# Seven value products from the third group on, and a late slot for three of four dense weight sums

## The chip, the cores and the metric

The kernel runs on one core of a Trainium2 chip. The metric is device time in microseconds (us) of one execution; three runs of the kernel before gave 767.40, 767.96 and 769.08 us, median 767.96 us.

## The reference

```python
def attention(x):                       # x is (2, 1024, 1024), already layer-normed
    x = conv1d(x, conv_w, width 3, 'SAME') + conv_b        # -> 3 * 256 columns
    q, k, v = split(x, 3); blocks of 128 tokens
    qh, kh, vh = q @ wq + bq, k @ wk + bk, v @ wv + bv      # 16 heads of 64
    p = softmax(causal(qh @ kh.T / 8))                      # within a block
    o = (p @ vh) @ wo + bo
    return o @ proj_w + proj_b
def ffn(x):                             # x is layer-normed again
    y = x @ W_base.T + b_base
    z = x @ A[active]; contribs = z @ B[active] * 2         # 4 active experts of rank 8
    alpha = softmax(log(prior + 1e-12) + x @ router_W.T + router_b)
    return y + sum(contribs * alpha)
x = x + attention(layernorm(x))
x = x + ffn(layernorm(x))
```

Everything is float32. All products are made so: an operand is split into a high part (`..._hi`, a rounded type that TensorE takes fast) and the rest (`..._lo`), and hi·hi, hi·lo and lo·hi are summed in PSUM.

## The kernel before

Up to about 250 us the convolution runs; from about 560 us on the second layer (the "dense" one) does. The change lies between them, in the attention.

The 2048 tokens are 8 **groups** of 256 tokens (e or g = 0 to 7), and the 16 heads are 8 pairs. A pair of heads in a group is a step jj; two of them are a **double step** D, `attention_pair(D)`, which every engine has as a function of its own. Group g owns the double steps 4g to 4g+3. Here ds 9 means D = 9. In a double step TensorE (PE) does, in this order: scores of two steps, head outputs of two older ones, transposes ("turns") of the probabilities, queries and keys of a new step, a *unit* (k = 0), queries and keys of the other step, a unit (k = 1), and the output sums. PE's matmuls of the scores (L2043) open a double step, so the time from one such start to the next is its length.

A *unit* is a part of the group's big products. In ds 4g+1 and 4g+2 the units are the **values** of group g (vh, a 256x256 by 256x1024 product); in ds 4g+3 and 4g+4 they are the output projection of group g-1, whose first matmul waits for `a_lo` of that group. The values exist in two forms, and the number `SEVEN` says from which group on the second is used:
- four units of two chunks each: 8 hi/lo products of three matmuls with 512 columns, 24 matmuls (`values`, L63 to L65);
- seven products of 2x2 blocks in place of eight, after Winograd's form of Strassen's scheme: 21 matmuls (`seven_values`, L1976 to L1978). Products 1 to 3 stand in ds 4g+1, 4 to 7 in ds 4g+2. VectorE adds them up into `vf` (L1455, L1458), and PE waits for its additions, since the seven share two PSUM banks.

The second form needs sums of blocks. For the values of group e VectorE makes four sums of the tokens' blocks in ds 4e-1 (`value_sums`, L1465 to L1470), ScalarE rounds them (`vs_hi`, L1043) and VectorE makes the rest (`vs_lo`, L1475) at the end of ds 4e. Once in the kernel GpSimd (POOL) makes four sums of the weight's blocks (`wv_again`, L800), ScalarE rounds them (`vt_hi`, L1061), and GpSimd makes the rest (`vt_lo`, L806), which product 3 of the first group of this form waits for (`pool_step` 10).

Beside it VectorE (DVE) prepares the sums of the dense layer's weights, 16 of them (k = 0 to 15): `weight_sum` (L1587) writes `t_raw`, ScalarE rounds it (`t_hi`, L1055), `low_sum` (L1599) makes the rest one sum later, and SyncE stores both to HBM. Sum k is due in double step 8 + 4(k/4) + (0, 0, 1, 2)[k mod 4]. In a double step VectorE has an early slot for it (after `heads_low`, L1430, ahead of the unit's additions) and a late slot (after the reciprocals and the units). Each engine works through its instructions in this written order.

GpSimd's other work here: the probabilities times the reciprocals (L784), the rest `c_lo` of the next group's tokens (L765, last in ds 4g+2 and 4g+3), and the bias sums of the residual (L775, two at the head of ds 4g+3). VectorE in ds 4g+3 first masks the scores of one step (L1418, four instructions), then makes `a_lo` (L1437), for which the projection on PE waits.

Of the kernel before, what the change touches and what calls it, by code (L numbers as in the profile page):

```python
# [19 lines left out]
WC = W // P  # L20
# [67 lines left out]
def network(nc, ident, x, conv_w, conv_b, wq, wk, wv, wo, pw, bq, bk, bv, bo, pb, w_base, b_base, lora_a, lora_b, router_w, router_b,  # L88
# [45 lines left out]
    DG = NP // 2  # L134
# [4 lines left out]
        e, n = ((g - 2, 2), (g, 0), (g, 2), (g - 1, 0))[q]  # L139
        return (q in (1, 2), e, n + k) if 0 <= e < NG else None  # L140

    SEVEN = 3

    def v_before(e):

        return VT * min(e, SEVEN) + 7 * max(0, e - SEVEN)

    def v_left(e, n, k):

        return v_before(e) + ((n + 1) if e < SEVEN else ((3, 2), (7, 6))[n // 2][k])  # L150

    def v_low(e):

        return WC + 5 * (e - SEVEN)

    def pair_of(D):

        return (2 * D, 2 * D + 1) if 0 <= D < ND else ()
# [26 lines left out]
    TFIRST, TSUMS = 8, 16  # L185
# [17 lines left out]
    def sum_at(k):  # L203
        return TFIRST + DG * (k // 4) + (0, 0, 1, 2)[k % 4]

    def sums_in(D, late):
        return [k for k in range(TSUMS) if sum_at(k) == D and (k % 4 == 1) == late]

    W_LAST = TFIRST + DG * (TSUMS // 4) + 1

# [40 lines left out]
    with ExitStack() as ctx:  # L251
# [135 lines left out]
        s = {n: sp.sem(n) for n in names}  # L387
# [55 lines left out]
        def value_raw(i):  # L443
            return value_block(*((0, 0), (0, 1), (1, 1), (1, 0))[i])

        def value_sum(part, i):
            return (vt_hi, vt_lo)[part][:, i] if i < 3 else (wv_hi, wv_lo)[part][:, 0, BANK:2 * BANK]
# [52 lines left out]
        def _(sync):  # L500
# [135 lines left out]
            def attention_step(g, i):  # L636
# [7 lines left out]
                if i == 7 and g + 2 < NG:  # L644
                    if g == 0:
                        sync.wait_ge(s["c_stored"], 16 * (MC + 1))
                    sync.wait_ge(s["c_lo_ready"], 2 * (g + 1))
                    if g + 1 >= SEVEN:
                        sync.wait_ge(s["v_low_step"], v_low(g + 1) + 4)
# [91 lines left out]
        def _(pool):  # L741
# [18 lines left out]
            def c_low(g, h):  # L760
                m = slice(3 * h, 3 * h + 3)
                pool.wait_ge(s["c_hi_ready"], 2 * (g - 1) + h + 1)
                wait(pool, s["qk_done"], NP * (g - 1))
                wait(pool, s["v_done"], v_before(g - 1))
                pool.tensor_tensor(c_lo[:, g % 2, m], c_raw[:, m], c_hi[g % 2][:, m], ALU.subtract).then_inc(s["c_lo_ready"], 1)  # L765

            def tile_power(t):
                pool.wait_ge(s["fvar_ready"], t + 1)
                r = rstd[:, t % 2] if t < BLOCKED else mv[:, t % 2, 1:2]
                pool.tensor_tensor(r, vareps[:, t % 2], mhalf[:], ALU.pow).then_inc(s["frstd_ready"], 1)  # L770

            def bias_sum(e, k):
                if k == 0:
                    pool.wait_ge(s["xr_loaded"], 16 * (e + 2))
                pool.tensor_tensor(xr[:, k], xr[:, k], pb_r[:], ALU.add).then_inc(s["xb_ready"], 1)  # L775

            def attention_pair(D):
                g, q = D // DG, D % DG
                if 0 <= g - 1 < NG - 1 and q == 3:
                    bias_sum(g - 1, 0)  # L780
                    bias_sum(g - 1, 1)
                for jj in pair_of(D - SC):
                    pool.wait_ge(s["rrec_ready"], jj + 1)
                    pool.tensor_tensor(pr[:, jj % 4], pr[:, jj % 4], rrec[:, jj % 4].unsqueeze(2).to_broadcast([P, UN, P]), ALU.mult).then_inc(s["p_ready"], 1)  # L784
                if 0 < g and g + 1 < NG and q in (2, 3):
                    c_low(g + 1, q - 2)
                if D == DG * SEVEN - 4:
                    value_weight_sums()
                if D == DG * SEVEN:
                    low_value_sums()  # L790
                if D in (27, 29):
                    tile_power((D - 27) // 2)

            def value_weight_sums():

                b11, b12, b21, b22 = (value_block(i, j) for i in range(2) for j in range(2))
                pool.wait_ge(s["wv_loaded"], 32)
                for k, (to, left, right) in enumerate(((b11, b12, b11), (b12, b22, b12), (b22, b22, b11), (b21, b21, b22))):
                    pool.wait_ge(s["pool_step"], 2 + k)
                    pool.tensor_tensor(to, left, right, ALU.subtract).then_inc(s["pool_step"], 1)  # L800

            def low_value_sums():

                for i in range(4):
                    pool.wait_ge(s["v_high_ready"], WC + i + 1)
                    pool.tensor_tensor(value_sum(1, i), value_raw(i), value_sum(0, i), ALU.subtract).then_inc(s["pool_step"], 1)  # L806

            pool.memset(mhalf[:], -0.5).then_inc(s["pool_step"], 1)
# [16 lines left out]
            for D in range(ND + 1):  # L825
                attention_pair(D)
# [57 lines left out]
        def _(act):  # L884
# [90 lines left out]
            def queries_keys(J):  # L975
                i = J % NP
                act.wait_ge(s["qk_done"], J + 1)
                wait(act, s["sc_done"], J - 1)
                act.activation(qf[:, J % 2], qk_acc(J)[:, 0], ACT.Identity, bias=bqk_c[:, 0, i:i + 1])
                act.activation(kf[:, J % 2], qk_acc(J)[:, 1], ACT.Identity, bias=bqk_c[:, 1, i:i + 1]).then_inc(s["qk_ready"], 1)  # L980
# [6 lines left out]
            def heads_out(jj):  # L987
                act.wait_ge(s["o_done"], jj // 2 * 2 + 2)
                wait(act, s["a_step"], jj - 1)
                act.activation(oT_hi[:, jj % 2], op[:, jj % 2].rearrange("p b t -> p (b t)"), ACT.Identity,  # L990
                               bias=bv_c[:, jj % NP:jj % NP + 1]).then_inc(s["oT_hi_ready"], 1)
# [11 lines left out]
            def a_high(e):  # L1003
                act.wait_ge(s["a_step"], NP * (e + 1))
                wait(act, s["yy_done"], YT * e)
                for d in range(WC):
                    a = act.activation(by_plane(a_hi[:, d]), planes_of(ap_[:, d]), ACT.Identity, bias=bo_c[:, d:d + 1])
                a.then_inc(s["a_hi_ready"], 1)

            def attention_pair(D):  # L1010
                g, q = D // DG, D % DG
                if q == 3 and 0 <= g - 1 < NG:
                    a_high(g - 1)
                for jj in pair_of(D - PV):
                    heads_out(jj)
                if D == 2:
                    queries_keys(2 * D)
                if D == ND:
                    exponentials(2 * (D - SC))
                for jj in pair_of(D - TR):  # L1020
                    turned_out(jj)
                for h in range(2):
                    if D < ND and D != 2 and h == 0:
                        queries_keys(2 * D)
                    if pair_of(D - SC) and (D, h) != (ND, 0):
                        exponentials(2 * (D - SC) + h)
                    if 0 < g and g + 1 < NG and (q, h) in ((1, 0), (3, 0)):
                        c_high(g + 1, q // 2)
                    if D < ND and D not in (2, 3, 4) and h == 1:
                        queries_keys(2 * D + 1)  # L1030
                if D == 2:
                    c_high(1, 0)
                    c_high(1, 1)
                for k in sums_in(D, False) + sums_in(D, True):
                    high_sum(k)
                if D == DG * SEVEN - 3:
                    high_value_sums(range(2))
                if D == DG * SEVEN - 1:
                    act.wait_ge(s["v_done"], v_before(SEVEN))
                    high_value_sums(range(2, 4))  # L1040
                if q == 3 and SEVEN <= g + 1 < NG:
                    act.wait_ge(s["v_low_step"], v_low(g + 1) + 4)
                    act.activation(vs_hi[:], vs_raw[:], ACT.Copy).then_inc(s["v_high_ready"], 1)  # L1043
                if D in (1, 2):
                    k = D - 1
                    act.wait_ge(s["wo_pw_loaded"], 32)
                    act.activation(wo_hi[:, 4 * k:4 * k + 4], wo_raw[:, 4 * k:4 * k + 4], ACT.Copy).then_inc(s["wo_hi_ready"], 1)
                if D in (4, 5):
                    act.wait_ge(s["wo_pw_loaded"], 32)
                    act.activation(pw_hi[:, D - 4], pw_raw[:, D - 4], ACT.Copy).then_inc(s["pw_hi_ready"], 1)  # L1050
# [6 lines left out]
            def high_value_sums(which):  # L1057

                for i in which:
                    act.wait_ge(s["pool_step"], 3 + i)  # L1060
                    act.activation(value_sum(0, i), value_raw(i), ACT.Copy).then_inc(s["v_high_ready"], 1)  # L1061
# [192 lines left out]
        def _(dve):  # L1254
# [216 lines left out]

            def low_values(e):

                dve.wait_ge(s["v_high_ready"], WC + 4 + e - SEVEN + 1)
                dve.tensor_tensor(vs_lo[:], vs_raw[:], vs_hi[:], ALU.subtract).then_inc(s["v_low_step"], 1)  # L1475

            def unit_out(D, k):
# [895 lines left out]
```

## Time and profile before

| | |
|---|---|
| median of 3 runs | 767.96 us |
| profiled execution | 767.93 us |
| its span | 766.2 us |
| clock granted to TensorE | 0.999 of full speed |
| PE busy | 745.9 us (97%) |
| VectorE busy | 584.6 us (76%) |
| ScalarE busy | 458.7 us (60%) |
| GpSimd busy | 186.1 us (24%) |
| DMA | 124.12 MB, mean 162 GB/s |

The span goes from the first to the last instruction; 1.7 us of the time lie around it. A row of a timeline gives start, duration, engine, line, operation, output and inputs, and in brackets how long the engine sat idle before and who released it. A recorded duration of VectorE includes what it waits inside the instruction.

### The profile page before, as it was taken

The page shows a single profiled execution, that of the slowest core. Times are in us where ns is not written, and L with a number is a line of the kernel's source. Part 1 is how long each engine was busy: PE and PEld are TensorE (multiplying, and loading weights), DVE is VectorE, ACT ScalarE, POOL GpSimd, SP SyncE. Part 2 cuts the span into 40 slices and gives each one's busy share as a digit, 9 for nine tenths or more (in the row PEclk, how much of TensorE's full clock was granted, in tenths as well). Part 3 has the DMA queues.
Part 4 walks back from the last instruction along what each step waited for, and adds up shares of the span by engine and source line. Part 5 has one row for each costly group of instructions (what it writes and reads, how often), then busy time and mean ns, then how long its engine had stood idle before and what let it go on. Part 6 is the DMA issues. An engine that isn't in the chain of part 4 may idle for free.

```text
span 766.2 us, 15175 instructions
## 1 busy us (share of the span) xinstructions
PE 745.9 (97%) x5311; PEld 670.7 (88%) x5311; DVE 584.6 (76%) x1573; ACT 458.7 (60%) x1189; POOL 186.1 (24%) x212
## 2 busy tenths in 40 slices
PE   4999999999999999999899999999999999999997
PEld 3898888888888889999899998999988899999997
DVE  6999996879888885767876776576688567777784
ACT  5963443334433787788677777777794155566530
POOL 2300100000000123645462626253430211222200
PEclk9999999999999999999999999999999999999999
DMA  8836843444445244163536364513357986433402
GB/s 323 300 119 188 259 118 130 173 165 145 165 143 215 111 167 118 56 205 104 177 101 212 89 218 155 188 48 111 114 195 224 353 219 208 134 124 134 159 29 83
DMA packets 64848, 124.12 MB, mean 162 GB/s; under 512 B 11908, under 2 KB 32516, under 8 KB 63365
## 3 DMA queue, kind: packets, MB, share of 16 engines
q1 hardware_dynamic: 62756, 115.81, 45.9%
q0 software_dynamic: 2016, 7.34, 2.4%
q8 instruction: 43, 0.70, 0.4%
q14 instruction: 33, 0.26, 0.1%
HBM read 87.92 MB, written 34.80 MB: 160 GB/s over the span
## 4 chain that ended last, share of the span: by engine, by line
PE 87%; DVE 5%; DMA 3%; ACT 3%; issue 1%; SPq 0%; DVEq 0%; ACTq 0%
PE net_psum L63 13%; PE net_psum L65 13%; PE net_psum L64 13%; PE net_psum L1941 11%; PE net_psum L2224 5%; PE net_psum L2226 5%; PE net_psum L2225 5%; PE net_psum L2043 4%; PE net_psum L2055 4%; PE net_psum L2067 3%; PE net_psum L2097 2%; PE net_psum L2098 2%; PE net_psum L2099 2%; DMA t_scratch<-t_low 1%; PE net_psum L1925 1%
## 5 line engine op out<-in xcount | busy, mean ns | idle before, releaser
L784 POOL TENSOR_TENSOR pr<-pr,rrec 128x512 f32<-128x512 f32 x64 | 66.5, 1042 | 195.3 <-DVE rrec L1426 194.2
L971 ACT ACTIVATE pr<-pr,negmax 128x128 f32<-128x128 f32 x256 | 99.6, 400 | 1.3 <-DVE negmax L1418 1.3
L1941 PE MATMUL net_psum<-ua,wa 128*128 128x256 f32 x384 | 83.8, 379 | 0.6 <-DVE ua L1308 0.6
L1941 PEld LDWEIGHTS net_psum<-ua,wa 128*128 128x128 f32 x384 | 72.6, 190 | 10.4 <-issue 0.8
L928 ACT ACTIVATE w_hi<-raw 128x1024 fp32r<-128x1024 f32 x24 | 25.5, 1063 | 85.4 <-PE net_psum L65 76.7
L63 PE MATMUL net_psum<-x_hi,w_hi 128*128 128x512 f32 x192 | 76.4, 398 | 0.0
L64 PE MATMUL net_psum<-x_lo,w_hi 128*128 128x512 f32 x192 | 76.2, 397 | 0.0
L65 PE MATMUL net_psum<-x_hi,w_lo 128*128 128x512 f32 x192 | 75.6, 394 | 0.0
L63 PE MATMUL net_psum<-c_hi,wqk_hi 128*128 128x256 f32 x256 | 74.1, 289 | 0.0
L64 PE MATMUL net_psum<-c_lo,wqk_hi 128*128 128x256 f32 x256 | 71.6, 280 | 0.0
L65 PE MATMUL net_psum<-c_hi,wqk_lo 128*128 128x256 f32 x256 | 71.5, 279 | 0.0
L1418 DVE CUSTOM_DVE_ANT_0 pr<-net_psum,mask 128x128 f32<-128x128 f32 x256 | 57.0, 285 | 19.0 <-PE net_psum L2043 19.0
L971 ACT ACTIVATION_READ_ACCUMULATOR pr<-pr,negmax 128x1 f32 x256 | 50.8, 199 | 0.0
L990 ACT ACTIVATE oT_hi<-net_psum,net_bv_c 128x256 fp32r<-128x256 f32 x64 | 26.9, 473 | 37.8 <-PE net_psum L2055 37.6
L64 PEld LDWEIGHTS net_psum<-c_lo,wqk_hi 128*128 128x128 f32 x256 | 48.2, 188 | 1.3
L63 PEld LDWEIGHTS net_psum<-c_hi,wqk_hi 128*128 128x128 f32 x256 | 48.1, 188 | 1.3
L65 PEld LDWEIGHTS net_psum<-c_hi,wqk_lo 128*128 128x128 f32 x256 | 48.1, 188 | 0.0
L1426 DVE RECIPROCAL rrec<-rsum 128x4 f32<-128x4 f32 x64 | 11.1, 175 | 47.5 <-ACT pr L971 47.4
L1750 DVE TENSOR_TENSOR x1t<-net_psum,x1t 128x528 f32<-128x528 f32 (+1 forms) x48 | 32.1, 690 | 15.8 <-PE net_psum L2226 14.7
L65 PEld LDWEIGHTS net_psum<-x_hi,w_lo 128*128 128x128 f32 x192 | 36.3, 189 | 8.6
L63 PEld LDWEIGHTS net_psum<-x_hi,w_hi 128*128 128x128 f32 x192 | 35.9, 187 | 8.9
L64 PEld LDWEIGHTS net_psum<-x_lo,w_hi 128*128 128x128 f32 x192 | 36.2, 188 | 8.4
(302 smaller groups left out, 2309.9 us busy)
## 6 DMA issues: line engine op xcount, KB each, us to landing
wa<-in_conv_w SPq DMA_DIRECT2D x24, 512.0 KB, 4.1
raw<-in_conv_w SPq DMA_DIRECT2D x24, 384.0 KB, 4.5
xn<-in_x SPq DMA_DIRECT2D x16, 512.0 KB, 10.5
xr<-in_x SPq DMA_DIRECT2D x8, 1024.0 KB, 5.6
x_scratch<-xr SPq DMA_DIRECT2D x8, 1024.0 KB, 4.5
x1t<-x_scratch SPq DMA_DIRECT2D x16, 512.0 KB, 4.9
x1g<-x_scratch SPq DMA_DIRECT2D x56, 128.0 KB, 3.0
out<-x1t POOLq DMA_DIRECT2D x14, 512.0 KB, 3.3
```

What stands on the lines that cost most here:

```text
L63: pe.matmul(out, w_hi, x_hi, start=first, stop=False)
L64: pe.matmul(out, w_hi, x_lo, start=False, stop=False)
L65: return pe.matmul(out, w_lo, x_hi, start=False, stop=last)
L784: pool.tensor_tensor(pr[:, jj % 4], pr[:, jj % 4], rrec[:, jj % 4].unsqueeze(2).to_broadcast([P, UN, P]), ALU.mult).then_inc(s["p_ready"], 1)
L971: e = act.activation(pr[:, jj % 4, un], pr[:, jj % 4, un], ACT.Exp, bias=negmax[:, jj % 2, un:un + 1], scale=-1.0, accum_out=rsum[:, jj % ...
L1418: m = dve.tensor_tensor_reduce(out=pr[:, jj % 4, un], in0=scp[:, h, jj % 2 * GT + b * P:jj % 2 * GT + (b + 1) * P], in1=mask[:], scale=-DH ...
L1750: dve.tensor_tensor(half_of(tile, j), bank_half(b, j), half_of(tile, j), ALU.add).then_inc(s["y_ready"], 1)
L1941: mm = pe.matmul(duo_acc(d, mi)[:, v * QUADS:(v + 1) * QUADS], wa[:, a % AW, mi, 1 - v, c % 2], ua[:, c, v, n * QUADS:(n + 1) * QUADS], st ...
L2043: mm = pe.matmul(scp[:, h, o], qf[e, jj % 2, t], kf[e, jj % 2, t], start=True, stop=True)
L2224: pe.matmul(to, x_hi, b_hi, start=c == 0 and o in (A11, S1, A12), stop=False, skip_group_check=True)
L2225: pe.matmul(to, x_hi, b_lo, start=False, stop=False, skip_group_check=True)
L2226: mm = pe.matmul(to, x_lo, b_hi, start=False, stop=c == DC // 2 - 1, skip_group_check=True)
```

## The change

Seven products now start with the third group (`SEVEN = 2`). The four GpSimd sums of the weight's blocks go from ds 8 to ds 7; their ScalarE roundings, two in ds 9 and two in ds 11 before, all stand at the end of ds 8, and GpSimd makes the low parts in ds 8 where it made them in ds 12. The waits are counted anew, since `vs_hi` of the third group now comes ahead of those roundings. And of the dense sums only k mod 4 = 0 keeps the early slot: k mod 4 = 2 and 3 (in ds 9, 10, 13, 14, 17, 18, 21 and 22) go to the late one, each with the `low_sum` that follows it.

```diff
--- before.py
+++ after.py
@@ -139,7 +139,7 @@
         e, n = ((g - 2, 2), (g, 0), (g, 2), (g - 1, 0))[q]
         return (q in (1, 2), e, n + k) if 0 <= e < NG else None
 
-    SEVEN = 3
+    SEVEN = 2
 
     def v_before(e):
 
@@ -204,7 +204,7 @@
         return TFIRST + DG * (k // 4) + (0, 0, 1, 2)[k % 4]
 
     def sums_in(D, late):
-        return [k for k in range(TSUMS) if sum_at(k) == D and (k % 4 == 1) == late]
+        return [k for k in range(TSUMS) if sum_at(k) == D and (k % 4 > 0) == late]
 
     W_LAST = TFIRST + DG * (TSUMS // 4) + 1
 
@@ -784,7 +784,7 @@
                     pool.tensor_tensor(pr[:, jj % 4], pr[:, jj % 4], rrec[:, jj % 4].unsqueeze(2).to_broadcast([P, UN, P]), ALU.mult).then_inc(s["p_ready"], 1)
                 if 0 < g and g + 1 < NG and q in (2, 3):
                     c_low(g + 1, q - 2)
-                if D == DG * SEVEN - 4:
+                if D == DG * SEVEN - 1:
                     value_weight_sums()
                 if D == DG * SEVEN:
                     low_value_sums()
@@ -802,7 +802,7 @@
             def low_value_sums():
 
                 for i in range(4):
-                    pool.wait_ge(s["v_high_ready"], WC + i + 1)
+                    pool.wait_ge(s["v_high_ready"], WC + 1 + i + 1)
                     pool.tensor_tensor(value_sum(1, i), value_raw(i), value_sum(0, i), ALU.subtract).then_inc(s["pool_step"], 1)
 
             pool.memset(mhalf[:], -0.5).then_inc(s["pool_step"], 1)
@@ -1033,11 +1033,9 @@
                     c_high(1, 1)
                 for k in sums_in(D, False) + sums_in(D, True):
                     high_sum(k)
-                if D == DG * SEVEN - 3:
-                    high_value_sums(range(2))
-                if D == DG * SEVEN - 1:
+                if D == DG * SEVEN:
                     act.wait_ge(s["v_done"], v_before(SEVEN))
-                    high_value_sums(range(2, 4))
+                    high_value_sums(range(4))
                 if q == 3 and SEVEN <= g + 1 < NG:
                     act.wait_ge(s["v_low_step"], v_low(g + 1) + 4)
                     act.activation(vs_hi[:], vs_raw[:], ACT.Copy).then_inc(s["v_high_ready"], 1)
@@ -1471,7 +1469,7 @@
 
             def low_values(e):
 
-                dve.wait_ge(s["v_high_ready"], WC + 4 + e - SEVEN + 1)
+                dve.wait_ge(s["v_high_ready"], WC + 1 if e == SEVEN else WC + 4 + e - SEVEN + 1)
                 dve.tensor_tensor(vs_lo[:], vs_raw[:], vs_hi[:], ALU.subtract).then_inc(s["v_low_step"], 1)
 
             def unit_out(D, k):
```

On VectorE the dense sum of ds 18 is one of the eight that move. From the outputs of the heads up to the first mask instruction of ds 19 its rows are, before:

```order
L1430 SCALAR_TENSOR_TENSOR oT_lo<-net_psum,net_bv_c,oT_hi 128x256 x2
L1455 COPY vf<-net_psum 128x512
L1587 TENSOR_TENSOR t_raw<-w_pair,t_raw 128x532
L1599 TENSOR_TENSOR t_low<-t_raw,t_hi 128x532
L1455 COPY vf<-net_psum 128x512
L1458 TENSOR_TENSOR vf<-net_psum,vf 128x512
L1426 RECIPROCAL rrec<-rsum 128x4 x2
L1458 TENSOR_TENSOR vf<-net_psum,vf 128x512
L1455 COPY vf<-net_psum 128x512
L1418 ISA pr,negmax<-net_psum,mask 128x128
```

And with the change (its line numbers are two lower here):

```order
L1428 SCALAR_TENSOR_TENSOR oT_lo<-net_psum,net_bv_c,oT_hi 128x256 x2
L1453 COPY vf<-net_psum 128x512 x2
L1456 TENSOR_TENSOR vf<-net_psum,vf 128x512
L1424 RECIPROCAL rrec<-rsum 128x4 x2
L1456 TENSOR_TENSOR vf<-net_psum,vf 128x512
L1453 COPY vf<-net_psum 128x512
L1585 TENSOR_TENSOR t_raw<-w_pair,t_raw 128x532
L1597 TENSOR_TENSOR t_low<-t_raw,t_hi 128x532
L1416 ISA pr,negmax<-net_psum,mask 128x128
```

The two dense instructions moved from the middle of ds 18 to its end, right ahead of the masks of ds 19.

On GpSimd the work on the weight's blocks moves. From the end of ds 7 on (the first `c_lo` row is its last instruction before the move) it has, before:

```order
L765 TENSOR_TENSOR c_lo<-c_raw,c_hi 128x768
L784 TENSOR_TENSOR pr<-pr,rrec 128x512 x2
L800 TENSOR_TENSOR wv_again<-wv_again 128x512 x4
L784 TENSOR_TENSOR pr<-pr,rrec 128x512 x4
L765 TENSOR_TENSOR c_lo<-c_raw,c_hi 128x768
L775 TENSOR_TENSOR xr<-xr,pb_r 128x1024 x2
L784 TENSOR_TENSOR pr<-pr,rrec 128x512 x2
L765 TENSOR_TENSOR c_lo<-c_raw,c_hi 128x768
L784 TENSOR_TENSOR pr<-pr,rrec 128x512 x2
L806 TENSOR_TENSOR vt_lo<-wv_again,vt_hi 128x512 x3
L806 TENSOR_TENSOR wv_lo<-wv_again,wv_hi 128x512
```

And with the change:

```order
L765 TENSOR_TENSOR c_lo<-c_raw,c_hi 128x768
L800 TENSOR_TENSOR wv_again<-wv_again 128x512 x4
L784 TENSOR_TENSOR pr<-pr,rrec 128x512 x2
L806 TENSOR_TENSOR vt_lo<-wv_again,vt_hi 128x512 x3
L806 TENSOR_TENSOR wv_lo<-wv_again,wv_hi 128x512
L784 TENSOR_TENSOR pr<-pr,rrec 128x512 x4
L765 TENSOR_TENSOR c_lo<-c_raw,c_hi 128x768
```

The block sums moved ahead of the two products of ds 8, and the low parts, which stood at the end of ds 12, right behind these two.

## Rows read from the trace of the kernel before

**Rows 1.** The page's chain that ended last, by engine
```profile
PE 87%; DVE 5%; DMA 3%; ACT 3%; issue 1%; SPq 0%; DVEq 0%; ACTq 0%
```

**Rows 2.** Timeline, PE: first scores of ds 9, 10, 13, 14, 17, 18, 19, 22, 23
```profile
323.66 0.38 PE L2043 MATMUL net_psum<-kf,qf 64*128 64x128 f32 x2
...
333.82 0.38 PE L2043 MATMUL net_psum<-kf,qf 64*128 64x128 f32 x2
...
364.23 0.38 PE L2043 MATMUL net_psum<-kf,qf 64*128 64x128 f32 x2
...
375.88 0.38 PE L2043 MATMUL net_psum<-kf,qf 64*128 64x128 f32 x2
...
406.30 0.38 PE L2043 MATMUL net_psum<-kf,qf 64*128 64x128 f32 x2
...
415.74 0.38 PE L2043 MATMUL net_psum<-kf,qf 64*128 64x128 f32 x2
...
426.06 0.38 PE L2043 MATMUL net_psum<-kf,qf 64*128 64x128 f32 x2
...
455.76 0.38 PE L2043 MATMUL net_psum<-kf,qf 64*128 64x128 f32 x2
...
466.80 0.38 PE L2043 MATMUL net_psum<-kf,qf 64*128 64x128 f32 x2
```

**Rows 3.** Timeline, end of ds 12, and product 3 in ds 13
```profile
363.96 1.27 POOL L806 TENSOR_TENSOR vt_lo<-wv_again,vt_hi 128x512 fp32r<-128x512 f32 x1
364.27 1.53 DVE L1587 TENSOR_TENSOR t_raw<-w_pair 128x532 f32<-128x532 f32 x1 [0.66 <-DMA t_scratch<-t_low]
365.73 1.80 DVE L1599 TENSOR_TENSOR t_low<-t_raw,t_hi 128x532 fp32r<-128x532 f32 x1
...
373.61 0.50 PE L1976 MATMUL net_psum<-vt_hi,vs_hi 128*128 128x512 f32 x1 [1.94 <-DVE vf L1455]
```

**Rows 4.** Timeline, DVE: the dense sum of ds 22
```profile
461.71 0.71 DVE L1587 TENSOR_TENSOR t_raw<-w_pair,t_raw 128x532 f32<-128x532 f32 x1 [1.15 <-DMA t_scratch<-t_low]
```

**Rows 5.** Timeline, ScalarE: its first work in ds 9, and two roundings
```profile
325.89 0.48 ACT L990 ACTIVATE oT_hi<-net_psum,net_bv_c 128x256 fp32r<-128x256 f32 x1 [1.18 <-PE net_psum L2055]
...
334.14 1.16 ACT L1061 ACTIVATE vt_hi<-wv_again 128x512 fp32r<-128x512 f32 x2
```

**Rows 6.** Timeline, ds 18: GpSimd's last product of probabilities, heads, PE's product 5
```profile
415.92 1.04 POOL L784 TENSOR_TENSOR pr<-pr,rrec 128x512 f32<-128x512 f32 x1 [0.93 <-DVE rrec L1426]
...
419.06 0.48 DVE L1430 SCALAR_TENSOR_TENSOR oT_lo<-net_psum,net_bv_c,oT_hi 128x256 fp32r<-128x256 f32 x1
...
421.11 0.39 PE L1976 MATMUL net_psum<-vt_hi,vs_hi 128*128 128x512 f32 x1
```

**Rows 7.** Timeline, from the end of ds 18 to the projection in ds 19
```profile
425.26 0.68 DVE L1455 COPY vf<-net_psum 128x512 f32<-128x512 f32 x1
425.83 1.82 POOL L765 TENSOR_TENSOR c_lo<-c_raw,c_hi 128x768 fp32r<-128x768 f32 x1
427.26 0.29 DVE L1418 CUSTOM_DVE_ANT_0 pr<-net_psum,mask 128x128 f32<-128x128 f32 x1 [1.32 <-PE net_psum L2043]
427.60 4.75 POOL L775 TENSOR_TENSOR xr<-xr,pb_r 128x1024 f32<-128x1024 f32 x2
428.11 1.55 DVE L1437 SCALAR_TENSOR_TENSOR a_lo<-net_psum,net_bcb_c,a_hi 128x128 fp32r<-128x128 f32 x4
430.52 0.40 PE L63 MATMUL net_psum<-pw_hi,a_hi 128*128 128x512 f32 x1
```

**Rows 8.** Timeline: near ties of VectorE and GpSimd at their SBUF operands
```profile
436.68 1.83 POOL L765 TENSOR_TENSOR c_lo<-c_raw,c_hi 128x768 fp32r<-128x768 f32 x1
436.74 1.79 DVE L1574 COPY w_pair<-a_raw 128x32 f32<-128x32 f32 x1
...
496.69 0.18 DVE L1574 COPY fw_raw<-a_raw 128x32 f32<-128x32 f32 x1
...
496.69 1.08 POOL L784 TENSOR_TENSOR pr<-pr,rrec 128x512 f32<-128x512 f32 x1 [1.24 <-DVE rrec L1426]
```

## The prediction

> **What bounds the kernel.** I read the page first, for the engine that ends last, then PE's timeline at the starts of the double steps, and then the other engines around each place where a double step is longer than its neighbours. The chain that ended last is 87% PE [rows 1]. PE sits idle for hardly anything in the attention, so its work there is worth its full time, and any wait added to it is paid. The starts of the scores [rows 2] give lengths: ds 9, with both units in the old form, takes 333.82 - 323.66 = 10.16 us; ds 17, with three products in place of four, 415.74 - 406.30 = 9.44; ds 18, 426.06 - 415.74 = 10.32. Two stand out: ds 13, the first with seven products, takes 375.88 - 364.23 = 11.65, 2.21 over ds 17, and ds 22 takes 466.80 - 455.76 = 11.04, 0.72 over ds 18. The change is to be judged by those two losses, by the third group's products, and by what its late slots run into.
>
> **Fewer matmuls, ds 9 and 10.** The third group's values lose three of 24 matmuls of 512 columns, all in ds 9. From 10.16 to the 9.44 of ds 17 that is -0.72, PE time on the path. Ds 18 is 0.16 longer than ds 9 although it has as many matmul columns; this follows a short ds 17, where PE is ahead of ScalarE's last queries and keys. I charge ds 10 the same +0.16. The adding up and the block sums cost VectorE three additions and five small operations more, in ds 7 to 10, where it has idle time; nothing.
>
> **The first group's stall, ds 13.** At the end of ds 12 GpSimd makes its four low parts while VectorE has a dense sum, a `low_sum` and `vs_lo`. VectorE's sum took 1.53 and its `low_sum` 1.80 [rows 3], against 0.71 for the same sum without GpSimd [rows 4]: they take turns. Where GpSimd ended its part at 363.96 + 1.27 = 365.23, VectorE's sum ended 0.57 later. VectorE comes to the masks of ds 13 late, then to an early dense sum and `low_sum` (0.71 recorded each [rows 4], 0.1 of it over the next one's start), and only then to the addition that PE waits for until 373.61 [rows 3]. With the change GpSimd is idle there and the early sum is gone: ds 13 becomes a ds 17, -2.21. Without the stall in front, ds 14 gets the 0.16 of ds 18 in its place: +0.16. Should half of the stall stay, the term would be -1.1.
>
> **The same work in ds 8 and 9.** The stall could come back where the weight's sums now stand. ScalarE is idle for 1.18 before 325.89 [rows 5], so it is free at 324.71. Four roundings follow; two took 1.16 [rows 5], so four take about 2.2 and end at 326.9, which puts its first work of ds 9 back by 1.0. GpSimd can start its low parts after the first rounding, at 325.3; uncontended they take 1.27 or less each [rows 3], so product 3 finds them at 330.4, and at 332.3 if each is held up as VectorE's were (1.75 each). In ds 13 PE had come to product 3 at 373.61 - 1.94 = 371.67, 7.44 after the start; in ds 9 that is 331.1. VectorE has no dense sum there any more before the end of ds 9, so I take the lower end, 330.4: no wait. ScalarE's lag is mostly taken up by its waits for PE: 0.1 for it. The far end is 332.3 - 331.1 = 1.2.
>
> **Ds 22.** The dense sum there waited 1.15 for the store of an earlier part [rows 4], and the unit's additions stood behind it. In the late slot it comes five us later, the store is done, and nothing of PE's is behind it: -0.72.
>
> **The late slot at the end of ds 9, 13, 17, 21** (k mod 4 = 2). VectorE begins the sum right after its last reciprocal, 0.2 ahead of GpSimd's product at 415.92 [rows 6]. So: sum 0.7, then GpSimd's 1.04 to 417.4, then `low_sum` to 418.0, and the masks of ds 18 start 0.8 later than they do. `heads_low` at 419.06 [rows 6] moves by less, since it waited for ScalarE: to about 419.6. Its 0.8 and the addition's 0.68 end at 421.1, and PE wants product 5 at 421.11 [rows 6]. I take 0.05 for each of ds 10, 14, 18, 22: +0.2; at most 0.3 each.
>
> **The late slot at the end of ds 10, 14, 18, 22** (k mod 4 = 3). This is the term that speaks against the change. VectorE's last addition begins at 425.26 and takes 0.68, of which the next instruction overlaps 0.08, so the dense sum is due at 425.86. There GpSimd starts 6.6 us without a gap: `c_lo` at 425.83 (1.82) and two bias sums from 427.60 (4.75) [rows 7]. Before, VectorE had nothing for them to hold up until the masks at 427.26, and `a_lo` from 428.11 to 429.66; PE takes it at 430.52 [rows 7]. The slack is 0.86. What follows depends on who has the operands first at 425.85:
> - VectorE first: sum to 426.55; `c_lo` held up by 0.6, to 428.25; `low_sum` 0.57 after it, to 428.82; the masks start at 428.75, 1.5 late. PE waits 1.5 - 0.86 = 0.64, and 0.1 to get going again: 0.74, four times 3.0.
> - GpSimd first: `c_lo` to 427.65; sum to 428.22; a bias sum of 2.38 to 430.6; `low_sum` to 431.15; the masks start at 431.1, 3.85 late: 3.85 - 0.86 + 0.1 = 3.1, four times 12.4.
>
> The margin is 0.03, and rows tell which side it falls on only roughly. At 496.69 both start, VectorE's copy takes its plain 0.18 and GpSimd's product 1.08 in place of 1.04: a tie by the record goes to VectorE. At 436.68 and 436.74 VectorE is 0.06 behind, and it is held for the whole of `c_lo` (1.79) [rows 8]. The change puts it 0.03 behind, between the two. Another copy of VectorE's stood just ahead of the one at 436.74, with GpSimd already in wait, so that loss need not repeat. I take VectorE first, as the nearer case, without much trust.
>
> The Trainium skill, page "SBUF — State Buffer", section "SBUF: two separate sides", has a rule for this: a VectorE operation with two SBUF inputs and a GpSimd operation that reads SBUF share a port pair, and whoever "starts first gets the pair for the whole instruction". The 1.80 of `low_sum` agrees. Applied to the recorded starts, 425.83 before 425.86, it gives the second case; the pair at 496.69 shows that the recorded start isn't quite the moment that decides.
>
> **The sum**, against the profiled execution's 767.93 (0.03 under the median of the runs): -0.72 (ds 9) +0.16 +0.1 (ds 10) -2.21 (ds 13) +0.16 (ds 14) -0.72 (ds 22) +0.2 (product 5) +3.0 (`a_lo`) = -0.03. I predict 767.9 us: 3.0 won and 3.0 lost. Other work is neither added nor moved on the path; the SyncE stores and loads of dense weights move back by some 4 us, and the weights of the next group are wanted 10 us after they could be loaded.
>
> **Rivals.**
> - *GpSimd first at the ends of ds 10, 14, 18 and 22.* The mechanism above, decided by 0.03 us at one place of a pattern that repeats. For it: the recorded order; against it: the tie at 496.69. Time: 767.93 - 3.03 + 12.4 = 777.3. If it falls so at some of the four only, each adds 2.4 to the forecast, 770 to 775.
> - *No collision.* If the two sums find the operands free, or `a_lo` has more slack than I read, only the gains stay: 767.93 - 3.03 = 764.9. For it: in ds 8 a late sum and `low_sum` (k = 1) stand beside GpSimd without a stall of PE. Against it: no projection waits for them there, and the bias sums are not beside them.
> - *The weights late in ds 9.* GpSimd's low parts, held up, end at 332.3: +1.2 on the forecast, 769.1. For it: rows 3; against it: VectorE has no dense sum beside them now.
>
> **Chances.** Forecast 0.40; GpSimd first everywhere 0.28, at some places 0.08; no collision 0.16; late weights 0.08. A difference under 0.2%, 1.5 us, is about what a measurement of this kernel can't tell from none: below 766.4 lie the third case and a tenth of the first (0.20), above 769.5 the GpSimd cases, a third of the late weights and a little of the first (0.42), between them 0.38. The forecast's own range is 766.4 to 769.5, since its gains are known to 0.5 and each of its eight waits to 0.2. For 8 times in 10 I need the gains alone on one side and most of the worst case on the other: 765.0 to 777.4.
>
> **What would show it.** In the profile after: ds 13 at 9.4 and ds 22 near 10.4 from scores to scores; ds 9 at 9.4 with product 3 not released by GpSimd; no VectorE sum over 1 us in ds 12. At the heads of ds 11, 15, 19 and 23 PE's projection released by `a_lo`, and the start of `a_lo` 3.6 us (VectorE first) or 5.9 us (GpSimd first) after the first scores, where it was 2.05. A late sum of 0.7 with `c_lo` at 2.4 means VectorE first; a sum of 2.4 with `c_lo` at 1.8 the rival. The prediction is wrong if ds 11, 15, 19, 23 keep their length, or if they grow by 3.

## The result, and the profile after

The changed kernel takes 781.32 us, median of four runs (781.08 to 781.76). The kernel before took 768.52 beside it (767.40 to 769.21, four runs). The ratio is 1.0169, 95% interval 1.0151 to 1.0186: slower by 1.7%, where I had forecast 767.9 and no change. The profiled execution has a span of 779.4, against 766.2.

Where did 13.2 us go? PE's timeline after: the first scores of ds 9, 10, 11, 12, 15 and 16 (the place of [rows 2]) and the four instructions for which it waited longest in the attention.

```profile
323.39 1.16 PE L2041 MATMUL net_psum<-kf,qf 64*128 64x128 f32 x16
333.19 1.48 PE L2041 MATMUL net_psum<-kf,qf 64*128 64x128 f32 x16
343.69 1.16 PE L2041 MATMUL net_psum<-kf,qf 64*128 64x128 f32 x16
350.99 0.47 PE L63 MATMUL net_psum<-pw_hi,a_hi 128*128 128x512 f32 x1 [2.67 <-DVE a_lo L1435]
356.71 1.16 PE L2041 MATMUL net_psum<-kf,qf 64*128 64x128 f32 x16
...
386.68 1.16 PE L2041 MATMUL net_psum<-kf,qf 64*128 64x128 f32 x16
393.92 0.47 PE L63 MATMUL net_psum<-pw_hi,a_hi 128*128 128x512 f32 x1 [2.62 <-DVE a_lo L1435]
401.24 1.16 PE L2041 MATMUL net_psum<-kf,qf 64*128 64x128 f32 x16
...
438.48 0.53 PE L63 MATMUL net_psum<-pw_hi,a_hi 128*128 128x512 f32 x1 [2.71 <-DVE a_lo L1435]
...
482.95 0.61 PE L63 MATMUL net_psum<-pw_hi,a_hi 128*128 128x512 f32 x1 [2.61 <-DVE a_lo L1435]
```

From start to start, in us:

| double step | before | after | difference |
|---|---|---|---|
| 9 | 10.16 | 9.80 | -0.36 |
| 10 | 10.15 | 10.50 | +0.35 |
| 11 | 10.12 | 13.02 | +2.90 |
| 13 | 11.65 | 9.43 | -2.22 |
| 14 | 10.15 | 10.39 | +0.24 |
| 15, 19, 23 | 10.14, 10.12, 10.15 | 14.56, 14.62, 14.52 | +13.29 |
| 22 | 11.04 | 10.39 | -0.65 |

The others kept their lengths within 0.03. The differences sum to +13.55, and ds 9 itself starts 0.27 earlier, which leaves the 13.3 by which the attention ends later. 3.2 us are won in ds 9, 13 and 22, 0.6 are lost in ds 10 and 14, and 16.2 at the four places where the projection waits for `a_lo`. The page's line on the chain says the same: DVE holds 7% of it, 5% before [rows 1].

```profile
PE 84%; DVE 7%; ACT 5%; issue 2%; DMA 0%; DVEq 0%; POOL 0%; ACTq 0%; POOLq 0%
```

The place itself, from the end of ds 14 to the projection in ds 15, all engines in one timeline. It answers to [rows 7].

```profile
386.31 1.81 POOL L765 TENSOR_TENSOR c_lo<-c_raw,c_hi 128x768 fp32r<-128x768 f32 x1
386.34 2.35 DVE L1585 TENSOR_TENSOR t_raw<-w_pair,t_raw 128x532 f32<-128x532 f32 x1
388.08 2.86 POOL L775 TENSOR_TENSOR xr<-xr,pb_r 128x1024 f32<-128x1024 f32 x1
388.62 2.89 DVE L1597 TENSOR_TENSOR t_low<-t_raw,t_hi 128x532 fp32r<-128x532 f32 x1
388.73 0.65 ACT L1053 ACTIVATE t_hi<-t_raw 128x532 fp32r<-128x532 f32 x1 [2.98 <-DVE t_raw L1585]
391.43 0.28 DVE L1416 CUSTOM_DVE_ANT_0 pr<-net_psum,mask 128x128 f32<-128x128 f32 x1
392.27 1.50 DVE L1435 SCALAR_TENSOR_TENSOR a_lo<-net_psum,net_bcb_c,a_hi 128x128 fp32r<-128x128 f32 x4
```

Read it from the left column. GpSimd's `c_lo` starts 0.03 before VectorE's sum, and runs its plain 1.81. The sum's recorded 2.35 ends at 388.69, 0.57 behind the end of `c_lo` (388.12): it had stood still through it. Then a bias sum takes its turn, slowed to 2.86, and `low_sum` stands behind that, to 391.51. The masks start at 391.43, and `a_lo` 5.59 after the scores where it was 2.05. This is the rival's sequence, instruction by instruction.

But the rival's price was 3.1 each, and three of the four double steps lost 4.4. A table by windows of the changed kernel (columns: length, PE busy, granted clock as a share of 2.4 GHz, DMA share, GB/s) has the double steps 11, 15, 19 and 23:

```profile
343.69:356.71 13.02, 10.35 (x89) 1.00 0.41 124
386.68:401.24 14.56, 11.94 (x89) 0.88 0.38 111
431.14:445.76 14.62, 11.91 (x90) 0.88 0.38 111
475.73:490.25 14.52, 11.91 (x90) 0.88 0.52 164
```

And the same microsecond by microsecond behind the wait in ds 15 (the clock is the value behind POOL's):

```profile
394.00:395.00 1.00, 1.00 (x4) 0.76 (x5) 1.00 (x8) 1.00 (x4) 0.00 (x0) 0.69 1.00 380
395.00:396.00 1.00, 1.00 (x4) 0.81 (x3) 0.99 (x4) 1.00 (x7) 0.00 (x0) 0.50 0.59 210
396.00:397.00 1.00, 1.00 (x5) 0.90 (x5) 0.83 (x2) 0.54 (x4) 0.00 (x0) 0.50 0.08 30
397.00:398.00 1.00, 1.00 (x8) 1.00 (x7) 0.30 (x3) 0.00 (x0) 0.68 (x1) 0.61 0.00 0
```

PE had been idle for 2.62 us up to 393.92; then the granted clock goes to 0.50, the 1.2 GHz level, and is on its way back by 398. PE's busy time in that double step is 11.94 where ds 11, with the same work, has 10.35: about 1.6 us of PE's own time. The page shows it too, once one knows: 96% of 779.4 us, and PE's busy sum is higher than before (745.9) although three matmuls fewer run.

```profile
PE 750.2 (96%) x5308; PEld 673.1 (86%) x5308; DVE 597.2 (77%) x1581; ACT 457.3 (59%) x1190; POOL 189.6 (24%) x212
```

### The profile page after: what moved, and what is told of

The parts are those of the page before. It is cut to its first block, busy times and chain, and to the rows that moved or that the text cites. A ratio compares the mean times of both kernels' runs of the same rounds, so it can differ in the third digit from the quotient of the medians.

```text
span 779.4 us, 15184 instructions
## 1 busy us (share of the span) xinstructions
PE 750.2 (96%) x5308; PEld 673.1 (86%) x5308; DVE 597.2 (77%) x1581; ACT 457.3 (59%) x1190; POOL 189.6 (24%) x212
## 4 chain that ended last, share of the span: by engine, by line
PE 84%; DVE 7%; ACT 5%; issue 2%; DMA 0%; DVEq 0%; POOL 0%; ACTq 0%; POOLq 0%
PE net_psum L63 13%; PE net_psum L65 13%; PE net_psum L64 13%; PE net_psum L1939 11%; PE net_psum L2222 5%; PE net_psum L2224 5%; PE net_psum L2223 5%; PE net_psum L2041 4%; PE net_psum L2053 3%; PE net_psum L2065 3%; ACT pr L971 3%; PE net_psum L2095 1%; PE net_psum L2096 1%; PE net_psum L2097 1%; DVE t_low L1597 1%
## 6 DMA issues: line engine op xcount, KB each, us to landing
xn<-in_x SPq DMA_DIRECT2D x16, 512.0 KB, 10.1
```

## The experiments

All times are medians, each with the ratio to the kernel before, run beside it on the same chip. Each edit is made to the changed kernel unless the text or a comment names another; the pieces of code are shortened to the lines that matter, and `...` stands for what is left out.

### The two halves of the change

**Seven products for the third group, dense sums as before.**

```diff
-    return [... and (k % 4 > 0) == late]
+    return [... and (k % 4 == 1) == late]
```

> Seven products from the third group on, as in the change, but the dense sums in the slots of before (only k mod 4 = 1 late). Theory A (the late slots at the ends of ds 10, 14, 18, 22 cost all of the loss: VectorE's dense sum and low_sum are blocked behind c_lo and a bias sum of GpSimd, a_lo comes late, PE waits): ds 11, 15, 19, 23 fall back to 10.1 us; ds 13 stays at 9.4; in ds 9 the early sum and low_sum now stand beside GpSimd's low parts and cost PE up to 1.5 us; in all about 767.6 us, at any rate within 2 us of before. Rival (the seven products of the third group, their sums and low parts cost it): still above 775 us.

Measured: 766.61 (765.95 to 767.26), ratio 0.9977 [0.9967, 0.9986]. Ds 11, 15, 19 and 23 keep 10.1; ds 13 is 9.44. So the new products and the place of the weight's sums have no part in the loss. Ds 9 is 11.11 here: the early dense sum and its `low_sum` stand ahead of the additions of the new unit, and beside GpSimd's low parts they take 1.32 and 1.80. (The early pair of ds 13 stands in the same place, takes 0.70 each, and costs nothing.) PE's timeline of ds 9:

```profile
332.52 0.50 PE L1974 MATMUL net_psum<-vt_hi,vs_hi 128*128 128x512 f32 x1 [1.05 <-DVE vf L1453]
```

**The late slot alone, four units for the third group.**

```diff
-    return [... and (k % 4 == 1) == late]      # the kernel before, SEVEN = 3
+    return [... and (k % 4 > 0) == late]
```

> The kernel before with the late slots for k mod 4 = 1, 2, 3 alone; seven products from the fourth group on. Theory A: ds 11, 15, 19, 23 grow as in the changed kernel, by 2.9 and three times 4.4 us, each with PE waiting 2.6 us for a_lo, ds 22 loses its 0.65, ds 13 loses the 1.2 us of its early sum and low_sum: about 782.5 us. Rival: the late slots alone cost less than half of the 12.8 us, under 775 us.

Measured: 778.84 (777.58 to 780.05), ratio 1.0132 [1.0116, 1.0148]. The late slot alone makes the loss: ds 15, 19 and 23 are 14.62 each in the profiled execution, the slowest of the four (777.58, 778.47, 779.21, 780.05, with a mean granted clock of 0.994, 0.994, 0.992 and 0.991). Ds 11 missed the expectation, at 10.72, and is the best row of the study. With the old units in ds 10 VectorE comes to its sum 0.42 ahead of `c_lo`. Timeline of this kernel, end of ds 10:

```profile
343.17 1.02 DVE L1587 TENSOR_TENSOR t_raw<-w_pair,t_raw 128x532 f32<-128x532 f32 x1
343.59 2.29 POOL L765 TENSOR_TENSOR c_lo<-c_raw,c_hi 128x768 fp32r<-128x768 f32 x1
344.12 2.33 DVE L1599 TENSOR_TENSOR t_low<-t_raw,t_hi 128x532 fp32r<-128x532 f32 x1
...
348.87 0.47 PE L63 MATMUL net_psum<-pw_hi,a_hi 128*128 128x512 f32 x1 [0.37 <-DVE a_lo L1437]
```

The sum goes first, `c_lo` is held (2.29 in place of 1.82), `low_sum` ends 0.57 after it, and the double step grows by 0.60. The sum takes 1.02 in place of 0.70, since GpSimd's product of probabilities runs until 343.63. That is the forecast's "VectorE first", which I had put at 0.74. Its size was nearly right; it only doesn't happen where the change puts the sum.

### Taking the collision away

**GpSimd's `c_lo` in ds 4g+2 waits for the late sum.** Nothing of VectorE's moves.

```diff
+                if q == 2:
+                    for k in sums_in(D, True):
+                        pool.wait_ge(s["t_step"], sum_step(k))
                 if 0 < g and g + 1 < NG and q in (2, 3):
                     c_low(g + 1, q - 2)
```

> The changed kernel, but GpSimd's c_lo at the end of ds 10, 14, 18, 22 waits until VectorE's late dense sum is done. Theory A says that who has the SBUF operands first decides: VectorE's sum takes 0.7 again, its low_sum follows at once, before GpSimd has seen the signal, the masks start on time and PE doesn't wait for a_lo: the 16.2 us of ds 11, 15, 19, 23 go, about 765.6 us. If the low_sum is still caught behind c_lo, the masks are 1.5 us late and PE waits 0.7 four times: 768.5. Rival (VectorE simply has 1.3 us too much work ahead of the masks, whoever is first): the stall stays over 2 us each time, above 775 us.

Measured: 765.33 (765.20 to 765.58), ratio 0.9961 [0.9948, 0.9975], 16 us under the changed kernel for a wait added on GpSimd. The timeline at the end of ds 14:

```profile
383.60 0.70 DVE L1588 TENSOR_TENSOR t_raw<-w_pair,t_raw 128x532 f32<-128x532 f32 x1
384.22 0.70 DVE L1600 TENSOR_TENSOR t_low<-t_raw,t_hi 128x532 fp32r<-128x532 f32 x1
384.38 2.24 POOL L765 TENSOR_TENSOR c_lo<-c_raw,c_hi 128x768 fp32r<-128x768 f32 x1 [0.77 <-DVE t_raw L1588]
...
388.40 0.39 PE L63 MATMUL net_psum<-pw_hi,a_hi 128*128 128x512 f32 x1
```

`low_sum` slips in as well, before GpSimd has woken; PE waits for nothing, and ds 15 is 10.1.

**A middle slot for k mod 4 = 3:** behind the unit's first additions and ahead of the reciprocals, three us sooner than the late one, with GpSimd idle.

```diff
                 unit_out(D, 0)
                 ...
+                weight_sums(D, MIDDLE_SLOT)        # k mod 4 == 3
                 for jj in pair_of(D - SC):
                     reciprocals(jj)
                 unit_out(D, 1)
                 ...
                 weight_sums(D, LATE_SLOT)          # k mod 4 == 1, 2
```

> The changed kernel with the sums of k mod 4 = 3 (ds 10, 14, 18, 22) between the unit's first additions and the reciprocals, where GpSimd is idle and VectorE has 1.3 us of idle time soon after. Theory A: all the gains, none of the stalls: ds 9 9.8, ds 13 9.4, ds 22 10.4, ds 11, 15, 19, 23 10.1: about 765.6 us, faster than before by 0.35%. Rival (the late sums of k mod 4 = 2, or the later reciprocals, cost PE as well): no faster than before, 768 us or more.

Measured: 765.30 (765.04 to 765.70), ratio 0.9961 [0.9947, 0.9975]. Ds 22 keeps its gain (10.38), and none of the four sums in the middle slot waits for a store. These two kernels beat both the kernel before and the changed one.

**Only k mod 4 = 2 late, k mod 4 = 3 early as before.**

```diff
-    return [... and (k % 4 > 0) == late]
+    return [... and (k % 4 in (1, 2)) == late]
```

> The changed kernel with k mod 4 = 3 back in the early slot of ds 10, 14, 18, 22; k mod 4 = 2 stays late. This is the smallest edit that takes away the collision. But sum k needs the buffer that the store of low part k-2 frees, and that store is now issued at the end of the double step before: it was issued 2.2 after the start of ds 18 in the kernel with the middle slot. Theory: the early sum waits for it, VectorE's additions behind it are late, and PE waits 1 to 2 in each of ds 10, 14, 18, 22: 769 to 773. Rival: the store is in time, and the kernel is as good as that with the middle slot, 765.3.

Measured: 765.92 (765.22 to 766.87), ratio 0.9975 [0.9965, 0.9985], close to the rival's 765.3 and far from the theory's 769 to 773. The wait for the store is there in two of the four double steps, but small; VectorE's sums of ds 14 and 18:

```profile
379.00 0.71 DVE L1585 TENSOR_TENSOR t_raw<-w_pair,t_raw 128x532 f32<-128x532 f32 x1 [0.36 <-DMA t_scratch<-t_low]
...
419.61 0.71 DVE L1585 TENSOR_TENSOR t_raw<-w_pair,t_raw 128x532 f32<-128x532 f32 x1 [0.57 <-DMA t_scratch<-t_low]
```

Ds 14 and 18 are 10.71 and 10.84, 0.3 and 0.5 over the middle slot; ds 10 and 22 are level with it. My 1 to 2 us each was at least twice too high. In ds 22 the early sum finds its store done (it starts at 459.68 without a wait), and the double step is 10.42 where it was 11.04: what the early slot cost there was the wait for the store, not the place.

### The clock after a wait of PE

**One late pair, in ds 14,** the others of k mod 4 = 3 in the middle slot.

```diff
-    return (EARLY_SLOT, LATE_SLOT, LATE_SLOT, MIDDLE_SLOT)[k % 4]
+    return LATE_SLOT if k == 7 else (EARLY_SLOT, LATE_SLOT, LATE_SLOT, MIDDLE_SLOT)[k % 4]
```

> The kernel with a middle slot (765.3), but sum 7 and its low_sum alone stand in the late slot of ds 14, where GpSimd's c_lo and two bias sums stand beside them. So there is one stall of PE of about 2.6 in place of four, at the head of ds 15. If one stall of that length is enough to bring the granted clock down for some us, ds 15 is 4.4 to 4.5 longer than in the kernel with the middle slot and the time about 769.7. If it takes the four together (the rival), or another thing is the cause, ds 15 is only 2.6 to 2.9 longer, and the time about 768.1.

Measured: 769.52, ratio 1.0017 [1.0007, 1.0027]. Of ten runs seven took 769.4 to 769.8 and three 768.1 to 768.2: both theories, by turns. The mean granted clock, recorded for every run, goes with it: 0.995 to 0.998 in the seven, 0.999 to 1.000 in the three. The profiled one is of the seven, its ds 15 14.57 long:

```profile
383.74:398.31 14.57, 11.90 (x89) 10.67 (x89) 11.67 (x37) 9.17 (x29) 10.94 (x6) 0.88 0.37 111
```

**One late pair, in ds 10** (the same edit with k == 3).

> As the kernel with one late pair in ds 14, but the one late pair is that of ds 10. In the changed kernel the granted clock stayed at 1.00 behind the stall in ds 11, though that was 2.67 like the others. If that belongs to the place, ds 11 is 2.9 longer than with the middle slot, with no stretch at the lower clock, and the time is about 768.2. If it was chance in the one profiled execution, the clock may fall here too: ds 11 4.4 longer, 769.7, or times spread between the two.

Measured: 769.55, ratio 1.0020 [1.0009, 1.0031]. Four runs took 767.9 to 768.3 (mean granted clock 0.998 to 1.000), five 769.5 to 769.7 (0.996 to 0.998), one 770.99 (0.994). The profiled one is of the four: PE waits 2.70, and the clock stays.

```profile
351.09 0.47 PE L63 MATMUL net_psum<-pw_hi,a_hi 128*128 128x512 f32 x1 [2.70 <-DVE a_lo L1451]
...
343.76:356.82 13.06, 10.36 (x89) 9.23 (x88) 11.71 (x35) 9.17 (x29) 9.68 (x6) 1.00 0.42 124
```

So, by the times and these clocks, it isn't the place. The same kernel, built to wait the same 2.7 us, falls to 1.2 GHz in some executions and not in others, and a fall costs 1.4 to 1.5 us. Only one execution of each kernel was profiled; that the slower runs of this one had the stretch at 0.50 is read from their times and mean clocks.

### What of the collision costs

**The sum stays late, its `low_sum` goes to the middle of the next double step.**

```diff
-                pair = [("sum", k, ...)] + ([("low", k - 1, ...)] if k else [])
+                pair = [("sum", k, ...)] + ([("low", k - 1, ...)] if k and k % 4 < 3 else [])
+            if k % 4 == 3 and sum_at(k) + 1 == D:
+                out.append(("low", k - 1, MIDDLE_SLOT))
```

> The changed kernel, but of the late pair in ds 10, 14, 18 and 22 only the dense sum stays; its low_sum goes to the middle of the next double step. If the price lies in the second instruction, which stands behind a bias sum of 2.4, then the sum alone, held for one c_lo, ends about 2.3 after it was due, the masks start 0.95 late and PE's wait for a_lo is 0 to 0.3: ds 11, 15, 19, 23 at 10.1 to 10.4, no stretch at the lower clock, 765.3 to 766.6. The rival, that the one blocked instruction is enough for most of the stall, gives a wait of more than 1 in each and 770 or more.

Measured: 769.75 (769.61 to 770.09), ratio 1.0025 [1.0015, 1.0036]: a miss. No fall of the clock, but PE waits 0.90 to 0.94 at each of the four places. ScalarE and PE at the end of ds 14 and in ds 15 of this kernel:

```profile
387.06 0.65 ACT L1071 ACTIVATE t_hi<-t_raw 128x532 fp32r<-128x532 f32 x1 [2.99 <-DVE t_raw L1604]
387.61 1.20 ACT L1025 ACTIVATE a_hi<-net_psum,net_bcb_c 128x256 fp32r<-128x256 f32 x2
388.84 1.53 DVE L1453 SCALAR_TENSOR_TENSOR a_lo<-net_psum,net_bcb_c,a_hi 128x128 fp32r<-128x128 f32 x4 [0.98 <-ACT a_hi L1025]
...
390.53 0.47 PE L63 MATMUL net_psum<-pw_hi,a_hi 128*128 128x512 f32 x1 [0.94 <-DVE a_lo L1453]
```

I had followed VectorE alone. ScalarE rounds the new sum (`t_hi`) as its last work of the double step, so it too waits for the held sum, 2.99 us, with `a_hi` queued behind it; and `a_lo` needs `a_hi`. There are two chains from the late sum to `a_lo`. In the changed kernel VectorE's is the longer one and hides this.

**The same, and `t_hi` of that sum stands behind `a_hi`.**

```diff
                 if q == 3 and 0 <= g - 1 < NG:
                     a_high(g - 1)
+                for k in sums_in(D - 1):
+                    if k % 4 == 3:
+                        high_sum(k)
```

> The kernel in which the low_sum of ds 10, 14, 18, 22 goes to the next double step (769.75), and ScalarE's rounding t_hi of the late sum stands behind its a_hi in place of ahead of it. New theory: the wait of 0.9 that was left in ds 11, 15, 19, 23 comes over ScalarE: t_hi waits for the held sum, a_hi stands behind it, and a_lo waits for a_hi. Then a_lo is bound by the masks alone, starts 2.8 to 2.9 after the scores (3.85 in that kernel), PE's wait for it is 0 to 0.1, and the time 765.2 to 765.8. Rival: the wait comes from VectorE, held for one c_lo, and stays at 0.9: 769.7.

Measured: 765.68 (765.49 to 765.84), ratio 0.9974 [0.9965, 0.9984], as the new theory had it. The timeline at the same place:

```profile
383.63 2.37 DVE L1608 TENSOR_TENSOR t_raw<-w_pair,t_raw 128x532 f32<-128x532 f32 x1
384.08 1.23 ACT L1025 ACTIVATE a_hi<-net_psum,net_bcb_c 128x256 fp32r<-128x256 f32 x2 [1.04 <-PE net_psum L2118]
386.04 0.65 ACT L1075 ACTIVATE t_hi<-t_raw 128x532 fp32r<-128x532 f32 x1 [0.73 <-DVE t_raw L1608]
386.77 1.54 DVE L1457 SCALAR_TENSOR_TENSOR a_lo<-net_psum,net_bcb_c,a_hi 128x128 fp32r<-128x128 f32 x4
```

The sum is held for the whole of `c_lo` as ever (2.37), and it costs only 0.1 to 0.2 in each double step (10.24 to 10.30 long).

**GpSimd's bias sums a double step earlier,** so that only `c_lo` stands there.

```diff
-                if 0 <= g - 1 < NG - 1 and q == 3:      # bias sums
+                if 0 <= g - 1 < NG - 1 and q == 2:
```

> The changed kernel, but GpSimd makes its bias sums a double step earlier (ds 4g+2 in place of 4g+3), so that behind c_lo it has nothing queued. The sum waits for c_lo (1.8), low_sum follows it at once, and the masks start 1.5 late: a wait of PE for a_lo of 0.7 in each of ds 11, 15, 19, 23, no fall of the clock, 768 to 769. If GpSimd's own c_lo is already enough for the whole stall (rival), the time stays near 781. If the bias sums in their new place, beside VectorE's work of ds 10, hold up something PE waits for, that shows as a wait in ds 10, 14, 18, 22.

Measured: 769.66 (769.47 to 775.02), ratio 1.0031 [1.0015, 1.0047], nearer to the theory's 768 to 769 than to the rival's 781, but above its range. The waits of PE are 0.74 to 0.94 without a fall of the clock; ds 11, 15, 19 and 23 take 11.1 to 11.3, and ds 30 is 0.4 longer, which I did not look into. One of its ten runs is the 775.02, which stays unexplained; without it the highest is 770.30. The bias sums are thus the larger part of the 2.9. In the rest `t_hi` has a part: `a_lo` waits a last 0.34 for `a_hi`.

```profile
386.74 0.70 DVE L1597 TENSOR_TENSOR t_low<-t_raw,t_hi 128x532 fp32r<-128x532 f32 x1
386.85 0.65 ACT L1053 ACTIVATE t_hi<-t_raw 128x532 fp32r<-128x532 f32 x1 [2.98 <-DVE t_raw L1585]
388.62 1.50 DVE L1435 SCALAR_TENSOR_TENSOR a_lo<-net_psum,net_bcb_c,a_hi 128x128 fp32r<-128x128 f32 x4 [0.34 <-ACT a_hi L1007]
```

## Why the prediction was wrong

**The step that failed** is in the term of the late slot at the end of ds 10, 14, 18 and 22: "I take VectorE first, as the nearer case, without much trust." The recorded start of GpSimd, 425.83, and the 425.86 worked out for VectorE decided as they stood. In the changed kernel and the experiments the late sum is recorded 0.02 to 0.04 behind `c_lo` in 20 cases, and GpSimd goes first in all 20 (the sum takes 2.35 to 2.37). In two cases it is recorded 0.38 and 0.42 ahead of `c_lo`, and it goes first; it takes 0.99 and 1.02 there, since GpSimd's product before `c_lo` still runs when it starts. I had set two near ties against each other [rows 8]; the tie at 496.69, which turned me to VectorE, has no difference in the record, so it could not say which side 0.03 falls on, while the copy at 436.74, 0.06 behind, was held.

The late slots of ds 9, 13, 17 and 21 show the other order. In 38 cases the sum is recorded 0.16 or 0.17 ahead of GpSimd's product of probabilities, takes its plain 0.70, and the product takes 1.43 or 1.44 in place of 1.04. Timeline of the changed kernel, end of ds 13:

```profile
376.30 0.70 DVE L1585 TENSOR_TENSOR t_raw<-w_pair,t_raw 128x532 f32<-128x532 f32 x1
376.46 1.44 POOL L784 TENSOR_TENSOR pr<-pr,rrec 128x512 f32<-128x512 f32 x1 [1.23 <-DVE rrec L1424]
```

The Trainium skill, page "SBUF — State Buffer", section "SBUF: two separate sides", has the rule that the one of the two that starts first holds the shared ports for its whole instruction. All 22 cases and these 38 agree, down to 0.02 us of recorded difference. I had cited it and then weighed one tie above it; the rule was the better guide.

**The margin could have been read as what it is.** At four places the same code runs with the same neighbours, so 0.03 is no coin to be thrown four times; it falls the same way at each. I gave all four together 0.28, which was at least a chance, but the likeliest case went to the wrong side.

**The second miss is in the rival's price.** By the lengths in ds 11 the collision costs 2.90, where I had 3.1. The account of 777.3 left out what PE's clock does after waits of 2.6 to 2.7 us: 4.42, 4.50 and 4.37 in ds 15, 19 and 23. Against the kernel with the middle slot: 765.30 + 4 x 2.9 + 3 x 1.5 = 781.4, measured 781.32. Without the clock it would have been 776.9, inside my range.

**The other terms, one by one.**
- Ds 13: -2.21 forecast, -2.22 measured. VectorE's sum of ds 12 takes 1.03 (1.53 in [rows 3]) and `low_sum` 0.70, since GpSimd has its low parts behind it. I had named two reasons, these low parts and the early sum of ds 13; the first is enough: with seven products alone, and that sum still early, ds 13 is 9.44 too. The late slot alone takes it to 10.41.
- Ds 22: -0.72 forecast, -0.65 measured.
- Ds 9: -0.72 forecast, -0.36 measured. The low parts are no cause: GpSimd ends them at 329.20 + 1.29 = 330.49 (forecast 330.4), and product 3 starts at 330.99 without a wait. ScalarE's four roundings end at 326.95 (forecast 326.9), and behind them lies most of the difference: its copies of the probabilities end at 328.65, and PE, which could have gone on with product 2 at 328.54 (its last matmul of product 1 starts at 328.31, and they follow each other by 0.23), starts it at 328.79. I had this lag as 0.1, in ds 10. That PE waits for these copies is read from the times; the profile names no releaser there. The kernel with the bias sums earlier bears it out: its copies end at 328.47, its product 2 starts at 328.72, 0.23 behind the matmul at 328.49, and its ds 9 takes 9.48, with a term of -0.68. Timeline after, ScalarE, GpSimd and PE:

```profile
324.77 1.66 ACT L1059 ACTIVATE vt_hi<-wv_again 128x512 fp32r<-128x512 f32 x3
326.33 0.62 ACT L1059 ACTIVATE wv_hi<-wv_again 128x512 fp32r<-128x512 f32 x1
327.57 1.08 ACT L996 ACTIVATE pT<-net_psum 128x512 f32<-128x512 f32 x2
328.79 0.47 PE L1974 MATMUL net_psum<-wv_hi,c_hi 128*128 128x512 f32 x1
329.20 1.29 POOL L806 TENSOR_TENSOR wv_lo<-wv_again,wv_hi 128x512 fp32r<-128x512 f32 x1
330.99 0.40 PE L1974 MATMUL net_psum<-vt_hi,vs_hi 128*128 128x512 f32 x1
```

- Ds 10: +0.26 and 0.05 forecast, +0.35 measured. Ds 14: +0.16 and 0.05 forecast, +0.24 measured. Ds 18: 0.05 forecast, 0.01 measured.

So the sum of the other terms, -3.03 forecast, came to -2.64, and nearly the whole error is the outcome of one race and the clock behind it. The late slot is worth having, for k mod 4 = 2: with that sum early, ds 9 is 1.3 longer. For k mod 4 = 3 it costs 16 us where it stands, and nothing that can be measured with one wait on GpSimd.

## What to carry to other kernels

Before an instruction is moved on VectorE, look at what GpSimd starts within a microsecond of its new place, and go by the recorded order, however close: 0.03 us decided 16 us here. Follow every engine that reads the moved result, since the one queued behind the wait may be a third engine. And a wait of PE of 2.6 us, as here, is to be priced with the 1.5 us that the clock may take behind it; where such a race can't be avoided, a wait on the engine with time to spare settles it.

## What the runs showed of the hardware

- A sum of VectorE that comes 0.03 after `c_lo` is held for the whole of it and ends 0.57 after it; its own time is 0.70. GpSimd's next operation then gets its turn ahead of VectorE's next, each slowed by the other (bias sum 2.86 in place of 2.38).
- The granted clock went to 0.50 for some 3.4 us, from within 1.1 us of PE's resuming after 2.6 to 2.7 us of idleness, in seven of the nine such waits that were profiled: in one kernel with one wait in seven runs of ten, by their times and mean clocks, in the other in six. The profiled waits of 0.37 to 1.05 (four kernels) and the one of 1.94 in the kernel before showed no fall, with a granted clock of 1.00 around them. What decides between two executions of the same kernel stays open.
- The kernel before has two clusters of times on its own: of the 30 runs of its longest series 16 lie at 767.0 to 767.7 and 12 at 768.3 to 769.0. The kernels with the wait on GpSimd, the middle slot, and `t_hi` behind `a_hi` have one, 0.4 to 0.7 wide. Their mean granted clocks differ as well: 0.998 to 1.000 in the 16, 0.995 to 0.998 in the 12. That points to some time at the lower clock in the slower cluster. That it comes from the wait of 1.94 in ds 13 [rows 3] would fit, but no profile caught it, so the place stays a guess. The kernel with only k mod 4 = 2 late has no such wait and 0.998 to 1.000 in all its runs; its spread of 1.65 has another cause, which is open.
